# Macaron block on one core: the state loops of a selective scan interleaved by group, the state sum moved from TensorE to GpSimd, the experts' weights streamed

## The chip, the cores and the metric

The kernel runs on one core of a Trainium2 chip. Its time is the device time of one execution in microseconds; the median of three runs before the change is 2610.5 us (2609.67 to 2610.94). The core has five instruction queues: TensorE (PE, matmuls; PEld is its weight load), VectorE (DVE), ScalarE (ACT), GpSimd (POOL) and SyncE (SP), which here issues every DMA. Each runs its own instructions in order and waits on semaphores for the others. SBUF is the on-chip memory, PSUM the eight banks that TensorE writes.

## The reference, cut to what matters

Input x is 16 sequences of 256 tokens, 128 channels, float32. Six parts follow one another, each added to x, each on a layer norm of x:

```
x = x + 0.5 * ffn_fp4(layernorm(x))        # 128 -> 352 -> 128, inputs and hidden values quantised in blocks of 16
x = x + mamba(layernorm(x))                # two layers
x = x + 0.5 * ffn_fp4(layernorm(x))
x = x + 0.5 * experts(layernorm(x))        # 8 experts, 128 -> 512 -> 128, each weighted by a gate
x = x + attention(layernorm(x))            # 16 heads of 8, causal, relative bias
x = x + 0.5 * experts(layernorm(x))

# one mamba layer, ED = 256 channels, N = 16 states each:
xi, z = split(rmsnorm(h) @ in_w.T);  u = silu(causal_conv4(xi))
dr, B, C = split(u @ xp_w.T);        delta = softplus(dr @ dtw.T + dtb)
for t in tokens:
    state = exp(delta[t] * A) * state + delta[t] * B[t] * u[t]      # [256, 16]
    y[t]  = sum over the 16 states of state * C[t]
h = h + ((y + Dp * u) * silu(z)) @ out_w.T
```

## The kernel before, in words

**Tiling.** The batch is cut into 8 groups of 2 sequences, 512 tokens each. A group's x lies in SBUF as [128, 4, 128]; a ring of XR = 5 groups is kept, and SP loads group g + 5 when group g is stored (`c_sp`). In the Mamba layers channels lie on the partitions and the 512 tokens along the row: 256 channels are two halves of 128.

**The state loop.** One pass is one layer of one group: 16 passes. Its loop has 32 steps (2 halves x 16 states). A step s is: TensorE spreads row B[s] over 128 partitions into PSUM (L748); VectorE multiplies it by delta * u (L700); ScalarE makes exp(delta * A) (L818); VectorE runs the recurrence over the tokens with one scan instruction into the ring `hst` of RS = 3 buffers (L706); SP has loaded row C[s] from DRAM, spread over 128 partitions, into the ring `cring` of RC = 4 (L849); GpSimd multiplies state by C into the ring `prod` of RP = 4 (L829), and after each odd step adds two products (L834). TensorE sums the eight pairs of a half in PSUM with identity matmuls (L758). A scan waits for the product three steps back, since they share a buffer of `hst`; the B row of a step waits for the scan two steps back.

**The way into a loop** (`mamba_dve`, `mamba_pe`, `mamba_act` ahead of the step loop): rms norm, transposes, in-projection (L727), convolution on VectorE (L629), u, silu(z), B and C rows (L732, B split into three bfloat16 parts), delta by softplus (L738, L659, L664, L673, L676) and delta * u (L680). It uses the three PSUM banks of lane a. **The way out** is `half_end` for each half, y + Dp * u from the PSUM sum (L686) times silu(z) (L690), then the out-projection (L764) and its addition to hm (L715); after layer 1, GpSimd adds hm to x (L1220). In a group all of this is one after the other: way in, loop, way out, layer by layer, and the next group's after it.

**Lanes.** Lane a is the Mamba part, group after group. Lane b is everything on the b banks, in `b_order` (L410 to L415): parts (0, g) and (1, g) are the two FFNs of group g, (2, g) its attention. Lane c is the two expert passes of each group in `moe_order` (L409 to L414). FFN quantisation is VectorE's (`quantize_dve`, L483 to L505); GpSimd does its last multiplication (L517). An expert pass has the up matmuls (L912), ScalarE's relu (L947), the down matmuls (L920), ScalarE's weighting (L955) and GpSimd's addition to x (L971), eight experts in turn.

**What sets the order.** Each lane is a Python generator that yields after each step, for each engine. `merge` (L118) draws steps from the lanes as a string tells it, written out for each engine (ORDER_PE, ORDER_DVE, ...): "b2d8b" is two steps of b, eight of d, one of b. On TensorE "d" is one warming matmul of 128 columns by the identity (`warm_pe`, L1351) into a bank of lane c; it may only stand where no expert pass is under way. ORDER_PE has 1816 of them. No engine can leave this order at run time.

**Weights.** `w1` and `w2` of all eight experts, 2 MB each, are loaded once at the start and stay in SBUF.

## Time and profile before

| | |
|---|---|
| median of three runs | 2610.5 us |
| profiled execution, its time | 2610.92 us |
| its span, first to last instruction | 2609.1 us |
| mean granted TensorE clock, share of full | 0.957 |
| busy: PE, DVE, ACT, POOL | 2392.5, 1866.3, 1559.5, 1368.1 us |
| GpSimd adds hm to x (a group leaves the Mamba part): first, last | 282.5, 2207.5 us |
| DMA moved | 175.30 MB, mean 67 GB/s |

A page of the profile is one execution. Busy time is the time in which an engine had an instruction under way. A group is all instructions of one line on one engine and shape; a group's row gives their busy time and the mean of one, then the engine's idle time just before them and what ended it. An fp32 matmul shows as two records, so L758's 512 records are 256 calls.

### The profile page before, as it was taken

What the parts mean: (1) busy time and instruction counts of PE and PEld (TensorE: products, weight loads), DVE (VectorE), ACT (ScalarE), POOL (GpSimd) and SP (SyncE); (2) the same over time, 40 slices, a digit from 0 to 9 for tenths busy, and PEclk for the clock granted to TensorE, in tenths of its full rate; (3) what the DMA queues carried; (4) which work ended last, traced back from release to release, by engine and by line L of the source; (5) the groups of instructions that cost most, each with busy time, mean ns of one, the idle gap of its engine ahead of it and who ended that gap; (6) DMA issues with size and microseconds to landing.
All of it is one profiled execution on the core that took longest, in us unless ns stands there. A gap on an engine that the chain in (4) does not pass through costs nothing.

```text
span 2609.1 us, 40448 instructions
## 1 busy us (share of the span) xinstructions
PE 2392.5 (92%) x14313; PEld 1680.7 (64%) x14313; DVE 1866.3 (72%) x3817; ACT 1559.5 (60%) x3377; POOL 1368.1 (52%) x1227
## 2 busy tenths in 40 slices
PE   7999997997898999889898989999898999988988
PEld 7878884685565666656565656666575656666675
DVE  5879797789587978698687968797879777322220
ACT  1424435543686558664886668665876685566654
POOL 1466483947373856558373847476564737212001
PEclk9999998998899999999899999999999999989999
DMA  4123131312220222112230222121311422100100
GB/s 152 56 76 108 48 97 37 101 46 85 79 90 31 82 86 93 37 63 76 90 90 30 89 86 86 41 79 65 105 54 58 126 60 71 34 20 1 49 5 5
DMA packets 97640, 175.30 MB, mean 67 GB/s; under 512 B 11957, under 2 KB 23133, under 8 KB 95646
## 3 DMA queue, kind: packets, MB, share of 16 engines
q1 hardware_dynamic: 97438, 172.71, 21.6%
q8 instruction: 113, 1.85, 0.3%
q14 instruction: 89, 0.73, 0.1%
HBM read 157.44 MB, written 15.23 MB: 66 GB/s over the span
## 4 chain that ended last, share of the span: by engine, by line
PE 66%; DVE 12%; ACT 11%; POOL 6%; issue 5%; DMA 0%; SPq 0%; POOLq 0%; DVEq 0%; ACTq 0%
PE c_bank L912 15%; PE c_bank L920 14%; PE c_bank L1351 8%; PE a_bank L758 7%; PE a_bank L748 3%; PE b_bank L1060 3%; DVE hst L706 2%; POOL prod_c L829 2%; PE a_bank L727 2%; PE b_bank L580 2%; PE b_bank L1050 1%; ACT weighted_y L955 1%; POOL prod_c L834 1%; PE b_bank L1099 1%; PE b_bank L561 1%
## 5 line engine op out<-in xcount | busy, mean ns | idle before, releaser
L829 POOL TENSOR_TENSOR prod_c<-hst,prod_c 128x512 f32<-128x512 f32 x512 | 670.9, 1318 | 382.0 <-DVE hst L706 362.4
L706 DVE TENSOR_TENSOR_SCAN hst<-dA,a_bank 128x512 f32<-128x512 f32 x512 | 621.1, 1213 | 9.6
L920 PEld LDWEIGHTS c_bank<-w,hid 128*128 128x128 f32 x4096 | 506.8, 196 | 75.7 <-ACT hid L947 38.6
L912 PE MATMUL c_bank<-c_xT,w 128*128 128x512 f32 x1024 | 534.4, 628 | 21.7 <-ACT hid L947 12.1
L920 PE MATMUL c_bank<-w,hid 128*128 128x128 f32 x4096 | 523.0, 280 | 7.6 <-ACT hid L947 7.5
L818 ACT ACTIVATE dA<-delta,a_neg 128x510 f32<-128x510 f32 x512 | 365.2, 719 | 269.1 <-DVE hst L706 260.4
L1351 PEld LDWEIGHTS c_bank<-ident 128*128 128x128 f32 x3632 | 439.1, 194 | 36.1 <-issue 27.2
L1351 PE MATMUL c_bank<-ident 128*128 128x128 f32 x3632 | 445.3, 277 | 1.7 <-ACT weighted_y L955 1.7
L947 ACT ACTIVATE hid<-c_bank,b 128x512 f32<-128x512 f32 x512 | 349.6, 687 | 150.8 <-PE c_bank L912 148.8
L971 POOL TENSOR_TENSOR xs<-xs,weighted_y 128x512 f32<-128x512 f32 x128 | 166.2, 1298 | 426.3 <-ACT weighted_y L955 424.7
L700 DVE TENSOR_TENSOR a_bank<-du,a_bank 128x512 f32<-128x512 f32 x512 | 348.5, 681 | 37.1 <-PE a_bank L748 35.6
L834 POOL TENSOR_TENSOR prod_c<-prod_c 128x512 f32<-128x512 f32 x256 | 341.1, 1332 | 15.4
L912 PEld LDWEIGHTS c_bank<-c_xT,w 128*128 128x128 f32 x1024 | 177.6, 196 | 207.4 <-ACT hid L947 95.7
L1017 DVE CUSTOM_DVE_ANT_0 att_buf<-b_bank,bias 128x256 f32<-128x256 f32 (+1 forms) x512 | 153.7, 353 | 203.6 <-PE b_bank L1050 198.5
L758 PE MATMUL a_bank<-prod_c,ident 128*128 128x512 f32 x512 | 276.0, 621 | 17.8 <-POOL prod_c L834 16.7
L748 PE MATMUL a_bank<-bc,sel 128*128 128x512 bf16 x512 | 199.3, 396 | 53.5 <-DVE hst L706 41.4
L955 ACT ACTIVATE weighted_y<-c_bank,gw 128x128 f32<-128x128 f32 x512 | 153.4, 367 | 143.6 <-PE c_bank L920 143.3
L1140 ACT ACTIVATE pT<-b_bank 128x384 f32<-128x384 f32 x256 | 125.0, 488 | 68.1 <-PE b_bank L1060 66.3
L1060 PEld LDWEIGHTS b_bank<-ident,att_buf 128*128 128x128 f32 x768 | 97.6, 150 | 99.8 <-issue 62.9
L1060 PE MATMUL b_bank<-ident,att_buf 128*128 128x128 f32 x768 | 137.3, 291 | 26.1 <-ACT pT L1140 15.9
L1131 ACT ACTIVATE att_buf<-att_buf,nmx 128x256 f32<-128x256 f32 x256 | 129.8, 507 | 29.6 <-DVE nmx L1017 29.2
L517 POOL TENSOR_TENSOR b_hq<-ffn_buf,b_quant_scales 128x704 f32<-128x704 f32 x32 | 44.9, 1404 | 190.6 <-DVE ffn_buf L505 190.6
(177 smaller groups left out, 2814.5 us busy)
## 6 DMA issues: line engine op xcount, KB each, us to landing
prod_c<-c_rows SPq DMA_DIRECT2D x512, 256.0 KB, 3.2
q_and_k<-qk_rows SPq DMA_DIRECT2D x64, 192.0 KB
qk_rows<-att_buf SPq DMA_DIRECT2D x40, 256.0 KB, 2.6
w<-in_w SPq DMA_DIRECT2D x2, 2048.0 KB
xs<-in_x SPq DMA_DIRECT2D x8, 256.0 KB, 6.7
bias<-skew SPq DMA_DIRECT2D x1, 2048.0 KB, 8.0
qk_rows<-b_xn SPq DMA_DIRECT2D x8, 256.0 KB, 3.0
out_dram<-xs SPq DMA_DIRECT2D x8, 256.0 KB, 2.4
```

Source lines behind the costliest of these rows:

```text
L700: nc.vector.tensor_tensor(b_bank, du[:, h, :], b_bank, ALU.mult).then_inc(M.dBx.sem, 1)
L706: nc.vector.tensor_tensor_scan(hst[:, s % RS, :], dA[:, s % RA, :], b_bank, 0.0, ALU.mult, ALU.add).then_inc(M.h.sem, 1)
L748: nc.tensor.matmul(S.bank[2 - s % 2 * 2][:, :], sel[:, s % NST, :], bc3[:, :], start=True, stop=True).then_inc(M.b.sem, 1)
L758: nc.tensor.matmul(S.bank[1][:, :], ident[:, :], prod[:, 2 * k % RP, :], start=(k % (NST // 2) == 0), stop=(k % (NST // 2) == NST // 2 - 1 ...
L818: nc.scalar.activation(half_batches(dA[:, s % RA, :], 1), half_batches(delta[:, h, :], 1), ACT.Exp, scale=a_neg[:, l, h, n:n + 1]).then_in ...
L829: nc.gpsimd.tensor_tensor(prod[:, s % RP, :], hst[:, s % RS, :], cring[:, s % RC, :], ALU.mult).then_inc(M.pp.sem, 1)
L834: nc.gpsimd.tensor_tensor(prod[:, (s - 1) % RP, :], prod[:, (s - 1) % RP, :], prod[:, s % RP, :], ALU.add).then_inc(M.pair.sem, 1)
L912: nc.tensor.matmul(S.bank[up_bank(e, c)][:, :], w1[:, e, c * 128:(c + 1) * 128], S.xT[:, :], start=True, stop=True).then_inc(M.up.sem, 1)
L920: ins = nc.tensor.matmul(S.bank[down_bank(f)][:, t * D:(t + 1) * D], hid[:, f % 2, j, t * 128:(t + 1) * 128], w2[:, f, j, :], start=(j == ...
L947: nc.scalar.activation(hid[:, e % 2, c, :], S.bank[up_bank(e, c)][:, :], ACT.Relu, bias=b1[:, e, c:c + 1]).then_inc(M.relu.sem, 1)
L1060: ins = nc.tensor.transpose(S.bank[2][:, j * 128:(j + 1) * 128], pr[:, m % 4, j * 128:(j + 1) * 128], ident[:, :])
L1351: nc.tensor.matmul(sc_.bank[0][:, 0:128], ident[:, :], ident[:, :], start=True, stop=True)
```

## The change

Lane a now holds only the state loops, numbered k = 0 to 15, in the order of `loops`: (0,0), (0,1), (1,0), (2,0), (1,1), (3,0), (2,1), ... (7,0), (6,1), (7,1), each (group, layer). So from the third loop on, neighbouring loops mostly belong to different groups. A new lane d holds the ways in ("gap") and out ("end"), in the order of `between`, and uses one PSUM bank, bank 1; a step there waits until the one before has been read. u, sz, delta, du and bc3 are doubled, hm is threefold, y has a tile of its own. The half-end of the second half moves from the loop to lane d. The softplus takes its maximum from PSUM before the logarithm is there.

The state sum: for each state after the first of a half GpSimd adds the product to `acc` in SBUF; the first is written there directly. The identity matmuls (L758) and the pair additions (L834) are gone, and `half_end` reads `acc` in place of a PSUM bank. RP is 3, XR is 6.

The experts' weights: `w1` and `w2` have two buffers of one expert each; SP loads 256 KB for each of both for every expert of all 16 expert passes (256 loads), each once the matmuls that used the buffer are done, drawn between the C rows by ORDER_SP, together with the stores and loads of x. b_order runs one FFN further ahead, (0, g + 3) in place of (0, g + 2).

All five order strings are new. ORDER_PE has 2181 warming calls (now "e"). After the last step of lane a, ORDER_PE had 157 steps of b, 272 of c and 97 warming calls; it has 209, 322 and 58.

The core of the diff; lines removed from functions that are printed above are mostly left out.

```diff
@@ -34,92 +34,98 @@
 EXP_MASK = 0x7F800000
 MAGIC = 1.5 * 2.0 ** 22
 BELOW = 1.0 - 2.0 ** -24
-XR = 5
+XR = 6
 PT = 6
-RS, RA, RP, RC = 3, 3, 4, 4
+RS, RA, RP, RC = 3, 3, 3, 4
+LOOPS = GROUPS * LAYERS
...
-        w1 = sb("w1", [128, EXPERTS, HID])
+        w1 = sb("w1", [128, 2, HID])
         b1 = sb("b1", [128, EXPERTS, HC])
-        w2 = sb("w2", [128, EXPERTS, HC, D])
+        w2 = sb("w2", [128, 2, HC, D])
...
-        yT = xc
+        yT = sb("yT", [128, HALVES, TOK])
+        acc = sb("y_sum", [128, HALVES, TOK])
...
-        b_order = [(0, 0), (0, 1), (1, 0), (0, 2)]
+        b_order = [(0, 0), (0, 1), (0, 2), (1, 0), (0, 3)]
         for g in range(1, GROUPS):
             moe_order += [(0, g), (1, g - 1)]
-            b_order += [(1, g), (0, g + 2), (2, g - 1)]
+            b_order += [(1, g), (0, g + 3), (2, g - 1)]
...
+        loops = [(0, 0), (0, 1), (1, 0)]
+        for g in range(2, GROUPS):
+            loops += [(g, 0), (g - 1, 1)]
+        loops.append((GROUPS - 1, 1))
...
+        def half_end(dve, L, M, k, h):
+            l, q = place(k)[1], k % 2
+            dve.wait_ge(M.acc.sem, L.at(M.acc, (h + 1) * (NST - 1)))
+            if h == 0 and k:
+                dve.wait_ge(M.proj.sem, k)
+            nc.vector.scalar_tensor_tensor(out=yT[:, h, :], in0=u[:, q, h, :], scalar=chan[:, 1, l, h:h + 1],
+                                           in1=acc[:, h, :], op0=ALU.mult, op1=ALU.add).then_inc(M.yD[h].sem, 1)
+            yield
+            dve.wait_ge(M.yD[h].sem, L.at(M.yD[h], 1))
+            nc.vector.tensor_tensor(yT[:, h, :], yT[:, h, :], sz[:, q, h, :], ALU.mult).then_inc(M.y[h].sem, 1)
+            yield
+        def loop_dve(dve, L, S, M, k):
+            q = k % 2
+            L.g = k
             for s in range(STEPS):
                 h, n = s // NST, s % NST
+                b_bank = S.bank[2 - s % 2 * 2][:, :]
+                if n == 0:
+                    dve.wait_ge(M.du.sem, L.at(M.du, h + 1))
                 dve.wait_ge(M.b.sem, L.at(M.b, s + 1))
+                nc.vector.tensor_tensor(b_bank, du[:, q, h, :], b_bank, ALU.mult).then_inc(M.dBx.sem, 1)
                 yield
                 dve.wait_ge(M.dBx.sem, L.at(M.dBx, s + 1))
                 dve.wait_ge(M.dA.sem, L.at(M.dA, s + 1))
+                if k * STEPS + s >= RS:
+                    dve.wait_ge(M.pp.sem, k * STEPS + s - RS + 1)
+                nc.vector.tensor_tensor_scan(hst[:, (k * STEPS + s) % RS, :], dA[:, (k * STEPS + s) % RA, :], b_bank, 0.0,
                                              ALU.mult, ALU.add).then_inc(M.h.sem, 1)
                 yield
+                if s == NST + 5:
+                    yield from half_end(dve, L, M, k, 0)
+        def end_dve(dve, L, S, M, k):
+            L.g = k
+            yield from half_end(dve, L, M, k, 1)
             dve.wait_ge(M.proj.sem, L.at(M.proj, 1))
+            nc.vector.tensor_tensor(hm[:, place(k)[0] % 3, :, :], hm[:, place(k)[0] % 3, :, :], S.bank[1][:, :].rearrange("p (t d) -> p t d", d=D),
                                     ALU.add).then_inc(M.added.sem, 1)
             yield
...
+            for j in range(4):
+                if 1 <= j <= 2:
+                    pe.wait_ge(M.conv.sem, L.at(M.conv, j))
+                elif j == 3:
+                    pe.wait_ge(M.sz.sem, L.at(M.sz, 1))
...
+        def loop_pe(pe, L, S, M, k):
+            L.g = k
             pe.wait_ge(M.bcS.sem, L.at(M.bcS, 1))
+            for s in range(STEPS):
+                if k * STEPS + s >= 2:
+                    pe.wait_ge(M.h.sem, k * STEPS + s - 1)
+                nc.tensor.matmul(S.bank[2 - s % 2 * 2][:, :], sel[:, s % NST, :], bc3[:, k % 2, :],
+                                 start=True, stop=True).then_inc(M.b.sem, 1)
+                yield
...
+        def loop_pool(pool, L, M, k):
+            L.g = k
+            def product(s):
+                h, n, i = s // NST, s % NST, k * STEPS + s
+                pool.wait_ge(s_c[i % RC], 16 * (i // RC + 1))
+                pool.wait_ge(M.h.sem, i + 1)
+                if n == 0 and k:
+                    pool.wait_ge(M.yD[h].sem, k)
+                if n > RP:
+                    pool.wait_ge(M.acc.sem, L.at(M.acc, h * (NST - 1) + n - RP))
+                elif n and h:
+                    pool.wait_ge(M.acc.sem, L.at(M.acc, NST - 1))
+                elif n and k:
+                    pool.wait_ge(M.acc.sem, 2 * (NST - 1) * k)
+                nc.gpsimd.tensor_tensor(prod[:, s % RP, :] if n else acc[:, h, :], hst[:, i % RS, :], cring[:, i % RC, :],
+                                        ALU.mult).then_inc(M.pp.sem, 1)
+                yield
+            def added(s):
+                h, n = s // NST, s % NST
+                if n:
+                    pool.wait_ge(M.pp.sem, L.at(M.pp, s + 1))
+                    done = h * (NST - 1) + n - 1
+                    if n > 1:
+                        pool.wait_ge(M.acc.sem, L.at(M.acc, done))
+                    nc.gpsimd.tensor_tensor(acc[:, h, :], acc[:, h, :], prod[:, s % RP, :], ALU.add).then_inc(M.acc.sem, 1)
+                    yield
+            for s in range(STEPS + 1):
+                if s < STEPS:
+                    yield from product(s)
+                if s:
+                    yield from added(s - 1)
+        def loop_sp(sp, L, M, k):
+            L.g = k
+            sp.wait_ge(s_cst, 16 * (k + 1))
             for s in range(STEPS):
+                i = k * STEPS + s
+                if i >= RC:
+                    sp.wait_ge(M.pp.sem, i - RC + 1)
+                row = bass.AP(c_dram.tensor, (k * NST + s % NST) * TOK, [[0, 128], [1, TOK]])
+                sp.dma_start(cring[:, i % RC, :], row).then_inc(s_c[i % RC], 16)
                 yield
...
+                        if c == 0:
+                            pe.wait_ge(s_w1[e % 2], 16 * ((L.g * EXPERTS + e) // 2 + 1))
+                        nc.tensor.matmul(S.bank[up_bank(e, c)][:, :], w1[:, e % 2, c * 128:(c + 1) * 128], S.xT[:, :],
...
         def c_sp(sp, L):
-            for g in range(GROUPS):
-                sp.wait_ge(moe.acc.sem, moe.acc.per * (moe_order.index((1, g)) + 1))
-                sp.dma_start(out[g * TOK:(g + 1) * TOK, :].rearrange("(t p) d -> p t d", p=128), x_of(g)).then_inc(s_out, 16)
-                yield
-                if g + XR < GROUPS:
-                    sp.wait_ge(s_out, 16 * (g + 1))
-                    load_x(sp, g + XR)
-                    yield
+            stored = 0
+            for n in range(EXPERTS * len(moe_order) + 2):
+                if n < EXPERTS * len(moe_order):
+                    if n >= 2:
+                        sp.wait_ge(moe.up.sem, HC * (n - 1))
+                    sp.dma_start(w1[:, n % 2, :], a["w1"][:, n % EXPERTS, :]).then_inc(s_w1[n % 2], 16)
+                    yield
+                    if n >= 2:
+                        sp.wait_ge(moe.down.sem, n - 1)
+                    sp.dma_start(w2[:, n % 2, :, :], a["w2"][:, n % EXPERTS, :, :]).then_inc(s_w2[n % 2], 16)
+                    yield
+                if n % EXPERTS == 1 and n > EXPERTS and moe_order[n // EXPERTS - 1][0]:
+                    g = moe_order[n // EXPERTS - 1][1]
+                    sp.wait_ge(moe.acc.sem, moe.acc.per * (n // EXPERTS))
+                    sp.dma_start(out[g * TOK:(g + 1) * TOK, :].rearrange("(t p) d -> p t d", p=128), x_of(g)).then_inc(s_out, 16)
+                    stored += 1
+                    yield
+                    if g + XR < GROUPS:
+                        sp.wait_ge(s_out, 16 * stored)
+                        load_x(sp, g + XR)
+                        yield
```

## Rows read from the trace of the kernel before

**Rows 1.** The page: busy us, share and instructions; the chain that ended last.
```profile
PE 2392.5 (92%) x14313; PEld 1680.7 (64%) x14313; DVE 1866.3 (72%) x3817; ACT 1559.5 (60%) x3377; POOL 1368.1 (52%) x1227
...
PE 66%; DVE 12%; ACT 11%; POOL 6%; issue 5%; DMA 0%; SPq 0%; POOLq 0%; DVEq 0%; ACTq 0%
```

**Rows 2.** Windows: PE, PEld, DVE, ACT, POOL busy us, PEclk, DMA share, GB/s.
```profile
0.00:98.00 98.00, 81.14 (x594) 72.69 (x595) 62.54 (x132) 31.80 (x70) 17.40 (x30) 1.00 0.34 113
98.00:2206.00 2108.00, 1948.91 (x11435) 1356.14 (x11434) 1713.30 (x3253) 1299.14 (x2777) 1287.60 (x1125) 0.96 0.24 74
2206.00:2609.00 403.00, 362.42 (x2289) 251.85 (x2287) 90.47 (x434) 228.56 (x531) 63.06 (x73) 0.94 0.07 19
450.00:500.00 50.00, 49.56 (x236) 30.79 (x236) 44.46 (x49) 32.79 (x62) 46.62 (x38) 0.99 0.37 111
600.00:650.00 50.00, 37.54 (x185) 24.17 (x184) 48.89 (x73) 18.37 (x33) 38.59 (x31) 0.86 0.28 84
1750.00:1800.00 50.00, 48.30 (x283) 35.03 (x282) 47.25 (x59) 25.16 (x54) 42.95 (x35) 1.00 0.25 79
```

**Rows 3.** Groups of the page: busy us, mean ns, idle before, releaser.
```profile
L829 POOL TENSOR_TENSOR prod_c<-hst,prod_c 128x512 f32<-128x512 f32 x512 | 670.9, 1318 | 382.0 <-DVE hst L706 362.4
L706 DVE TENSOR_TENSOR_SCAN hst<-dA,a_bank 128x512 f32<-128x512 f32 x512 | 621.1, 1213 | 9.6
L912 PE MATMUL c_bank<-c_xT,w 128*128 128x512 f32 x1024 | 534.4, 628 | 21.7 <-ACT hid L947 12.1
L920 PE MATMUL c_bank<-w,hid 128*128 128x128 f32 x4096 | 523.0, 280 | 7.6 <-ACT hid L947 7.5
L1351 PE MATMUL c_bank<-ident 128*128 128x128 f32 x3632 | 445.3, 277 | 1.7 <-ACT weighted_y L955 1.7
L700 DVE TENSOR_TENSOR a_bank<-du,a_bank 128x512 f32<-128x512 f32 x512 | 348.5, 681 | 37.1 <-PE a_bank L748 35.6
L834 POOL TENSOR_TENSOR prod_c<-prod_c 128x512 f32<-128x512 f32 x256 | 341.1, 1332 | 15.4
L758 PE MATMUL a_bank<-prod_c,ident 128*128 128x512 f32 x512 | 276.0, 621 | 17.8 <-POOL prod_c L834 16.7
```

**Rows 4.** Windows of L1351 alone: PE and PEld busy us.
```profile
98.00:2206.00 2108.00, 362.90 (x2958) 358.93 (x2959) 0.96 0.24 74
2206.00:2609.00 403.00, 24.11 (x193) 22.43 (x191) 0.94 0.07 19
```

**Rows 5.** Timeline of POOL in a loop alone: start us, us.
```profile
257.85 2.50 POOL L829 TENSOR_TENSOR prod_c<-hst,prod_c 128x512 f32<-128x512 f32 x2
...
260.43 1.27 POOL L834 TENSOR_TENSOR prod_c<-prod_c 128x512 f32<-128x512 f32 x1
```

**Rows 6.** Window from loop 0's end to loop 1's first step, as rows 2.
```profile
184.00:211.00 27.00, 26.90 (x189) 22.45 (x188) 13.56 (x21) 16.66 (x33) 1.21 (x2) 1.00 0.12 41
```

**Rows 7.** Waits: us in total, times, longest us.
```profile
POOL prod_c L829 <- DVE hst L706: 362.4, 169, 27.0
...
DVE xc L686 <- PE a_bank L758: 45.7, 12, 5.9
...
POOL prod_c L829 <- DMA prod_c<-c_rows: 14.3, 2, 11.0
```

**Rows 8.** Timeline of two SBUF inputs beside POOL, and L492's shortest, median, longest.
```profile
335.43 1.27 POOL L829 TENSOR_TENSOR prod_c<-hst,prod_c 128x512 f32<-128x512 f32 x1 [0.72 <-DVE hst L706]
...
335.76 1.68 DVE L492 TENSOR_TENSOR ffn_buf<-att_buf,b_quant_scales 128x704 f32<-128x704 f32 x1
336.77 1.80 POOL L834 TENSOR_TENSOR prod_c<-prod_c 128x512 f32<-128x512 f32 x1
...
L492 DVE TENSOR_TENSOR ffn_buf<-att_buf,b_quant_scales x32: 860/892/1952, 39.1 to 2243.1; 128x704 f32<-128x704 f32 x32
```

**Rows 9.** SP's loads of the C rows: issue ns, and us to landing.
```profile
L849 SPq DMA_DIRECT2D prod_c<-c_rows x512: 319/320/854, 88.6 to 2188.7; - x171
...
DMA to landing us min/median/max: 2.9/3.2/11.3
```

More of the change, by code:

```diff
@@ L288, in build @@
         s_cst = plain("c_rows_in_dram")
+        s_w1 = [plain(f"up_weights_loaded_{i}") for i in range(2)]
+        s_w2 = [plain(f"down_weights_loaded_{i}") for i in range(2)]
         s_qkd = plain("q_and_k_in_dram")
@@ L616, in half_batches, with place, gaps_and_ends @@
             return ap.rearrange("p (b s) -> p b s", b=GB)[:, :, k:]
-        def mamba_dve(dve, L, S, M, l):
-            N = M.norm
-            step = [0, 0]
-            for k in range(1, KCONV):
-                for h in range(HALVES):
-                    if k == 1:
+        loops = [(0, 0), (0, 1), (1, 0)]
+        for g in range(2, GROUPS):
+            loops += [(g, 0), (g - 1, 1)]
+        loops.append((GROUPS - 1, 1))
+        def place(k):
+            return loops[k]
+        def gaps_and_ends():
+            todo, ended = [], 0
+            for k, (g, l) in enumerate(loops):
+                due = max(k - 1, loops.index((g, 0)) + 1 if l else 0)
+                while ended < due:
+                    todo.append(("end", ended))
+                    ended += 1
+                todo.append(("gap", k))
+            return todo + [("end", k) for k in range(ended, LOOPS)]
```

532 lines of the change are left out of this document (264 added, 268 removed).

## The prediction

> **What bounds the kernel now.** The page first: TensorE is busy 2392.5 of 2609.1 us and has 66% of the chain that ended last [rows 1]. The groups then say what that busy time is: 445.3 us of it are the warming matmuls of L1351, which no result needs, and 276.0 us the state sum of L758 [rows 3]. So TensorE is full, but not with work. The windows show three parts [rows 2]: a way in until the first scan (98 us), the stage of the state loops (98 to 2206 us), and a tail of 403 us with neither scan nor GpSimd product, where TensorE is busy 362.4 us. In the stage VectorE is busy 1713.3 of 2108 us (81%), GpSimd 1287.6 (61%), TensorE 1948.9, less 362.9 of warming [rows 4], that is 75% with work.
>
> A state loop with nothing beside it runs at GpSimd's pace: two products in 2.50 us and a pair addition to 1.27 us, 3.8 us for two steps [rows 5]; VectorE needs 0.68 + 1.21 us a step [rows 3]. Between two loops of a group VectorE is busy 13.56 us and GpSimd 1.21 us of the 27 us from 184 to 211 [rows 6]: that is the gap which the change fills. In the stage GpSimd waits 362.4 us for the state, and VectorE 45.7 us for the last state sum [rows 7].
>
> **The change, part by part.** I sum over the stage, as a bill for each engine, and put the first loop and the tail beside it. There are 16 passes (loop with its ways in and out).
>
> *State sum off TensorE.* 256 calls (512 records of L758) go: 276.0 us of busy time. On GpSimd 256 pair additions become 30 additions in each pass, 480 in all: 224 more of 1.27 us, 285 us. Its stage bill goes from 1287.6 to 1573 us. A pass then has 32 products and 30 additions, 62 x 1.27 = 79 us, where it had 48, 61 us.
>
> *Interleaving.* From pass 2 on, a pass's way in belongs to another group and can lie under the loop before it. Nothing is removed by that; it allows VectorE to go from 81% to what its dense stretches reach: 48.89 of 50 us (98%) from 600, 47.25 (95%) from 1750 [rows 2]. Pass 1 still needs pass 0 of the same group, so one gap stays open: 27 us [rows 6], 30 us with all ways in on one bank, where each matmul now waits for the reader of the one before. Elsewhere I cost this longer chain at nothing, since a loop of 80 us or more covers it; bare, it would cost at most VectorE's idle time of such a gap once more, 27 - 13.56 = 13 us a pass, up to 215 us in all [rows 6].
>
> *SBUF inputs beside GpSimd.* This is the cost that decides. While GpSimd is inside a product, a VectorE operation with two SBUF inputs waits: L492 takes 1.68 us at 335.76 beside L829, and 0.86 at its shortest; the GpSimd addition behind it then takes 1.80 us in place of 1.27 [rows 8]. A pass has 29 such operations: 10 in the way in, 4 on the way out (L686 now reads the sum from SBUF and not from PSUM), 15 in an FFN's quantisation. Before, the ways in and much of the FFN ran while GpSimd stood idle. If GpSimd is busy 85% of the time, and the wait is on average half of its 1.27 us, that is 29 x 0.85 x 0.64 = 16 us a pass, less some 4 us that the mean durations hold already (L829 and L834 are 0.05 us over 1.27 in the mean, and VectorE's share is like it): 12 us, 195 us in all. The bounds: 0 (the orders place them where GpSimd waits) and 29 x 0.82 = 24 us, less 4: 320 us (each as at 335.76). I take 195, between them. GpSimd loses as much again.
>
> The Trainium skill has this as a rule ("SBUF — State Buffer", section "SBUF: two separate sides"): VectorE with two SBUF inputs and GpSimd share one port pair under an exclusive lock held for a whole instruction, so that the loser blocks fully. The trace agrees (1.68 us against 0.86, rows 8). The rule speaks against this change, since it moves work onto GpSimd and VectorE's SBUF operations beside it.
>
> *The stage's sum.* VectorE: 1713.3, less 26 us of attention work that moves into the tail, plus 195: 1882 us. At 96% (between the 95 and the 98 above) 1960 us, plus the open gap of 30: 1990. GpSimd would have 1573 + about 200 in it, 89%; it reached 46.62 of 50 us (93%) from 450 [rows 2], so VectorE bounds, narrowly. TensorE with work: 1586 less 276 less 62, 63%: free.
>
> *Tail.* Counted in the written orders, TensorE has after the last state-loop step now 4 expert passes, 2 attentions and an FFN (272 and 157 steps); after the change 322 and 209, with 58 warming calls in place of 97, so 50 of the 68 steps of one expert pass and 52 of the 70 of an attention more, and 39 calls fewer. An expert pass is (534.4 + 523.0) / 16 = 66 us [rows 3]; the tail's 362.4 us less four of them less 24.1 of warming [rows 2, 4] leave 74 for two attentions and an FFN, some 30 each. So 66 x 50/68 + 30 x 52/70 - 39 x 0.245 = 62 us, at the tail's share (90%) 69. Tail 472 us. Below, 30 us if it fills idle time; above, 85.
>
> *Streamed weights.* 256 loads of 256 KB replace two of 2 MB. SP issues one in 0.32 us, such a load lands in 3.2 us [rows 9], and a buffer comes free one expert (66/8 = 8 us) before its use. Cost 0 when SP is on time. But SP is one queue in order: a load that waits for an expert's matmul holds the C rows behind it, of which the ring has four, 4 x 2.53 = 10 us. Bounds 0 and 11.3 - 3.2 = 8 us (its longest landing) for a third of the 128 experts, 340 us; I take 0, the nearest row being that products waited for this queue only twice in 512 [rows 7]. With fewer bytes before it the way in is shorter or the same; a third group's FFN goes into it: 98 becomes 100 us.
>
> **Sum.** 100 + 1990 + 472 = 2562 us of span; the profiled execution took 1.8 us more than its span and is 0.4 above the median of 2610.5. I say 2560.
>
> **Rivals.**
> (a) *The forecast*, VectorE bound with lock waits: 2560, own range 2510 to 2605. Chance 0.38.
> (b) *The waits for the port stay small and the overlap holds*: VectorE 1687 us at 94% (the 95% stretch) 1795, plus 30; 100 + 1825 + 472 = 2397. TensorE gives the same: 2392.5 - 276.0 + 365 more warming calls in the new order x 0.245 = 2206 us, at the present 92% 2405. For it: from 1750 VectorE, GpSimd and TensorE are all near full together (47.25, 42.95, 48.30 of 50) [rows 2]. Against: rows 8. With all between it and (a), 2390 to 2510: 0.22.
> (c) *GpSimd becomes the bound*: 79 us of loop, (1287.6 - 1012) / 16 = 17 of other work, 29 x 0.85 x 0.89 = 22 of waiting for VectorE's SBUF operations, 118 us a pass. VectorE waits for the product three steps back, and GpSimd for the scan, so each one's stall returns to the other. At the 86% of the stretch from 1750 that is 137 us a pass, 2195 + 30, in all 2797; at 90%, 131 us, 2700. It decides once a pass takes over (2609 - 100 - 472 - 30) / 16 = 125 us, that is GpSimd under 94% with these waits. For it: GpSimd never stood above 93% [rows 2]. Against: the waits are counted on both sides, while one side's wait frees the other. I give it 2620 to 2720, chance 0.30. By the skill's rule alone, with every one of the 29 blocked, this would be the outcome; its time is the one given here.
> (d) *SP's queue starves the products*: a third of the 128 experts at 8 us, of which half is covered: 2560 + 170 = 2730. Chance 0.05. (e) *The overlap doesn't come about* because the orders, written for other durations, make each way in wait: the gap of 27 us stays in half of the passes, 2560 + 7 x 27 = 2750, of which 130 falls away again (two thirds of the 195, since GpSimd then idles): 2620. Chance 0.05.
>
> **How the numbers follow.** The likeliest single case is (a), so 2560. Faster holds (b) and nearly all of (a), 0.59; within 0.2% (5 us, about what a measurement of this kernel can tell from no change) 0.07, from the edges of (a), (c) and (e); slower 0.34, (c), (d) and a little of (a). The range for 8 in 10 runs from the middle of (b), 2440, to 2690, which leaves out the upper end of (c). Both signs hold much of the chance; (a)'s own range stands above.
>
> **What would show it.** L758 and its idle times gone; an addition on GpSimd of 480 records. Mean durations of the VectorE operations with two SBUF inputs (L492, L501, L664, L680, L690) well above those before, and of GpSimd's products above 1.32 us: 12 us a pass in sum for (a), next to none for (b). VectorE at 94% or more of the stage with the first and last scan some 1990 us apart. For (c) GpSimd is above 90% and VectorE's waits are for products; for (d) products wait for the C rows; for (e) VectorE waits for its ways in. The tail should take 472 us. The prediction is wrong if TensorE's chain still ends the stage, if the port costs nothing, or if the tail grows by less than 30 us.

## The result: slower, with the profile after

The changed kernel takes 2673.4 us (median of 4 runs, 2668.7 to 2683.9) against 2610.2 us (the kernel before, now four runs): a ratio of 1.0245 [1.0231, 1.0258], 63 us slower. The forecast was 2560 us, so faster.

The page after gives busy us, share and instructions, then the chain that ended last. It answers to [rows 1].
```profile
PE 2296.8 (86%) x14381; PEld 1678.7 (63%) x14531; DVE 1948.8 (73%) x3817; ACT 1572.8 (59%) x3387; POOL 1672.6 (63%) x1451
...
PE 46%; DVE 19%; ACT 12%; issue 9%; POOL 5%; DMA 1%; another core or an unknown queue 0%; SPq 0%; POOLq 0%; DVEq 0%; ACTq 0%
```
TensorE's part of the chain fell from 66% to 46%, and no single engine took its place: VectorE has 19%. The windows after, with the columns of [rows 2]: the way in, the stage, the tail, then the stretch between the first and the last scan in two parts (from the first scan of pass 0 to the first of pass 6, and from there to the last scan), and three stretches of the early part.
```profile
0.00:114.00 114.00, 95.45 (x713) 86.23 (x716) 74.11 (x157) 35.27 (x81) 21.30 (x36) 1.00 0.24 72
114.00:2195.00 2081.00, 1769.47 (x10911) 1295.13 (x11057) 1761.70 (x3100) 1256.91 (x2641) 1573.98 (x1331) 0.92 0.32 98
2195.00:2671.00 476.00, 431.91 (x2760) 297.37 (x2759) 112.97 (x564) 280.60 (x668) 77.30 (x85) 0.94 0.19 57
111.50:806.50 695.00, 562.29 (x3550) 442.24 (x3599) 620.95 (x799) 312.28 (x582) 552.71 (x449) 0.88 0.27 81
806.50:2197.80 1391.30, 1211.94 (x7393) 856.45 (x7490) 1144.77 (x2311) 948.14 (x2069) 1024.65 (x888) 0.94 0.35 106
550.00:600.00 50.00, 23.31 (x77) 12.91 (x78) 38.79 (x45) 20.67 (x43) 44.33 (x40) 0.60 0.35 99
600.00:650.00 50.00, 30.03 (x99) 15.05 (x100) 46.34 (x48) 21.46 (x36) 44.43 (x35) 0.64 0.35 107
650.00:700.00 50.00, 16.82 (x39) 6.83 (x39) 46.86 (x58) 21.17 (x42) 43.53 (x37) 0.53 0.24 74
```
The kernel before, cut at the same two places:
```profile
98.30:843.10 744.80, 689.94 (x4268) 517.07 (x4266) 608.05 (x996) 371.83 (x750) 448.89 (x387) 0.96 0.24 73
843.10:2195.10 1352.00, 1248.45 (x7088) 829.80 (x7089) 1102.15 (x2253) 924.73 (x2021) 832.11 (x732) 0.96 0.25 76
```
From 550 to 700 GpSimd is busy 44 of 50 us and TensorE 17 to 30, at a granted clock of 0.53 to 0.64. Over the whole stage VectorE is busy 1761.7 of 2081 us, 84.7%. In [rows 2] it was 81%; 96% were forecast.

For a split that needs no choice of borders, take each kernel's first and last scan (name, ns at least/median/most, start of the first to start of the last). Before:
```profile
L706 DVE TENSOR_TENSOR_SCAN hst<-dA,a_bank x512: 1152/1220/1222, 98.3 to 2195.1; 128x512 f32<-128x512 f32 x171
```
After:
```profile
L760 DVE TENSOR_TENSOR_SCAN hst<-dA,a_bank x512: 1153/1212/1223, 111.5 to 2197.8; 128x512 f32<-128x512 f32 x171
```
The way in is 13.2 us longer, the stretch from first to last scan 10.5 us shorter (2086.3 against 2096.8), and what follows the last scan 59.5 us longer (473.5 against 414.0): +62.2 of span. So the tail came near its forecast (+69), and the stage didn't shrink by 118 us but by some 10. These 10 us are a difference of two parts: passes 0 to 5 became 50 us shorter (695 against 745), passes 6 to 15 became 39 us longer (1391 against 1352). VectorE's idle time between the same marks fell from 137 to 74 us in the early passes. In the late passes it did not fall (250 and 246 us), while VectorE's busy time there rose by 43 us. So the new lanes filled VectorE's idle time in the early passes only.

The groups that answer to [rows 3]:
```profile
L935 POOL TENSOR_TENSOR prod_c<-hst,prod_c 128x512 f32<-128x512 f32 x480 | 644.1, 1343 | 221.2 <-issue 169.9
L946 POOL TENSOR_TENSOR y_sum<-y_sum,prod_c 128x512 f32<-128x512 f32 x480 | 647.2, 1348 | 1.6
L760 DVE TENSOR_TENSOR_SCAN hst<-dA,a_bank 128x512 f32<-128x512 f32 x512 | 619.7, 1210 | 38.7 <-POOL prod_c L935 26.5
L1036 PE MATMUL c_bank<-c_xT,w 128*128 128x512 f32 x1024 | 544.3, 638 | 26.1 <-ACT weighted_y L1080 12.8
L1463 PE MATMUL c_bank<-ident 128*128 128x128 f32 x4362 | 540.2, 279 | 13.8 <-DVE hst L760 11.8
L1045 PE MATMUL c_bank<-w,hid 128*128 128x128 f32 x4096 | 504.6, 277 | 7.9 <-ACT hid L1072 6.3
```
L758 is gone, and L946 has 480 records, as the change says.

### The profile page after: what moved, and what is told of

It reads as the page before. It is cut to its first block, busy times and chain, and to the rows that moved or that the text cites. A ratio compares the mean times of both kernels' runs of the same rounds, so it can differ in the third digit from the quotient of the medians.

```text
span 2671.3 us, 41985 instructions
## 1 busy us (share of the span) xinstructions
PE 2296.8 (86%) x14381; PEld 1678.7 (63%) x14531; DVE 1948.8 (73%) x3817; ACT 1572.8 (59%) x3387; POOL 1672.6 (63%) x1451
## 4 chain that ended last, share of the span: by engine, by line
PE 46%; DVE 19%; ACT 12%; issue 9%; POOL 5%; DMA 1%; another core or an unknown queue 0%; SPq 0%; POOLq 0%; DVEq 0%; ACTq 0%
PE c_bank L1036 13%; PE c_bank L1045 13%; DVE hst L760 6%; PE c_bank L1463 4%; DVE a_bank L754 3%; PE b_bank L1185 3%; POOL y_sum L946 2%; ACT weighted_y L1080 2%; PE a_bank L792 1%; ACT dA L900 1%; PE b_bank L1175 1%; POOL prod_c L935 1%; PE b_bank L592 1%; ACT hid L1072 1%; PE b_bank L1224 1%
## 5 line engine op out<-in xcount | busy, mean ns | idle before, releaser
L935 POOL TENSOR_TENSOR prod_c<-hst,prod_c 128x512 f32<-128x512 f32 x480 | 644.1, 1343 | 221.2 <-issue 169.9
L946 POOL TENSOR_TENSOR y_sum<-y_sum,prod_c 128x512 f32<-128x512 f32 x480 | 647.2, 1348 | 1.6
L760 DVE TENSOR_TENSOR_SCAN hst<-dA,a_bank 128x512 f32<-128x512 f32 x512 | 619.7, 1210 | 38.7 <-POOL prod_c L935 26.5
L1036 PE MATMUL c_bank<-c_xT,w 128*128 128x512 f32 x1024 | 544.3, 638 | 26.1 <-ACT weighted_y L1080 12.8
L1463 PE MATMUL c_bank<-ident 128*128 128x128 f32 x4362 | 540.2, 279 | 13.8 <-DVE hst L760 11.8
L1463 PEld LDWEIGHTS c_bank<-ident 128*128 128x128 f32 x4362 | 533.5, 196 | 24.1 <-issue 16.6
L1045 PEld LDWEIGHTS c_bank<-w,hid 128*128 128x128 f32 x4096 | 485.2, 193 | 56.9 <-ACT hid L1072 38.8
L1045 PE MATMUL c_bank<-w,hid 128*128 128x128 f32 x4096 | 504.6, 277 | 7.9 <-ACT hid L1072 6.3
L1142 DVE CUSTOM_DVE_ANT_0 att_buf<-b_bank,bias 128x256 f32<-128x256 f32 (+1 forms) x512 | 152.1, 353 | 230.7 <-PE b_bank L1175 230.2
L816 PE MATMUL a_bank<-bc,sel 128*128 128x512 bf16 x362 | 148.5, 418 | 137.8 <-DVE hst L760 133.5
L816 PEld LDWEIGHTS a_bank<-bc,sel 128*128 128x128 bf16 x512 | 51.0, 100 | 248.3 <-DVE hst L760 205.8
```

What stands on the lines that cost most here:

```text
L760: nc.vector.tensor_tensor_scan(hst[:, (k * STEPS + s) % RS, :], dA[:, (k * STEPS + s) % RA, :], b_bank, 0.0, ALU.mult, ALU.add).then_inc(M ...
L816: nc.tensor.matmul(S.bank[2 - s % 2 * 2][:, :], sel[:, s % NST, :], bc3[:, k % 2, :], start=True, stop=True).then_inc(M.b.sem, 1)
L935: nc.gpsimd.tensor_tensor(prod[:, s % RP, :] if n else acc[:, h, :], hst[:, i % RS, :], cring[:, i % RC, :], ALU.mult).then_inc(M.pp.sem, 1)
L946: nc.gpsimd.tensor_tensor(acc[:, h, :], acc[:, h, :], prod[:, s % RP, :], ALU.add).then_inc(M.acc.sem, 1)
L1036: nc.tensor.matmul(S.bank[up_bank(e, c)][:, :], w1[:, e % 2, c * 128:(c + 1) * 128], S.xT[:, :], start=True, stop=True).then_inc(M.up.sem, 1)
L1045: ins = nc.tensor.matmul(S.bank[down_bank(f)][:, t * D:(t + 1) * D], hid[:, f % 2, j, t * 128:(t + 1) * 128], w2[:, f % 2, j, :], start=(j ...
```

## The experiments

Kernels whose labels begin with e are the changed kernel with one edit, those with b are the kernel before with one edit. "The time" is the median, set against the 2673.4 of the changed kernel for e and against the kernel before of the same chip (2610.0 to 2611.4) for b. Four theories on where the stage's gain went are named in the expectations. Q: loads of weights hold up the C rows in SP's queue. P: GpSimd, by its longer loop and the SBUF port that it shares with VectorE, sets the pace. I: GpSimd paces the early passes, TensorE's experts the late ones and the tail. O: no engine bounds alone; the written orders do.

**e1_no_stream.** The streaming taken away: two experts' weights are loaded once and serve all eight.
```diff
-                    if n >= 2:
-                        sp.wait_ge(moe.up.sem, HC * (n - 1))
-                    sp.dma_start(w1[:, n % 2, :], ...)
+                    if n < 2:
+                        sp.dma_start(w1[:, n % 2, :], ...)
```
(and so for w2; TensorE waits only for the first load of each buffer.)


> Changed kernel without the streaming: two experts' weights are loaded once and serve all eight (the other six experts' weights are left out), so SP issues no load that waits for an expert's matmul. Theory Q (SP's one queue in order: a weight load that waits holds the C rows behind it, and GpSimd stands idle 191 us before its products with no releaser shown): most of these 191 us go, the idle time named issue before L935 falls below 40 us, and the time falls by 100 to 190 us, to 2490 to 2570. Theory P (the port and GpSimd's load): GpSimd idles elsewhere instead, time within 20 us of 2673. Theory O (the written orders fit none of the real durations, so a stall removed in one place returns in another): 10 to 60 us less.


Measured: 2663.8 us (2660.2 to 2674.0), 1.0211 [1.0188, 1.0233] of before, 10 less than the changed kernel, which is at the edge of what these runs can tell apart. In the changed kernel SP waits behind experts' down matmuls for 598.9 us in 121 waits, and it costs next to nothing. GpSimd's waits before its products, 169.9 us marked "issue" in the changed kernel, stay. Changed kernel (us in total, times, longest us):
```profile
POOL prod_c L935 <- issue: 169.9, 72, 12.9
...
SPq L1488 <- PE c_bank L1045: 598.9, 121, 11.9
```
and without streaming:
```profile
POOL prod_c L935 <- issue: 167.8, 72, 12.4
```
Rival (d) falls. The trace also says what these waits are, the longest one first (start us, us):
```profile
784.30 1.21 DVE L760 TENSOR_TENSOR_SCAN hst<-dA,a_bank 128x512 f32<-128x512 f32 x1
785.65 1.77 POOL L935 TENSOR_TENSOR prod_c<-hst,prod_c 128x512 f32<-128x512 f32 x1 [12.86 <-issue]
```
Each of the 77 products before which the idle time is marked "issue" (the 72 above and five that write `y_sum`, 191 us together) starts 0.13 to 0.14 us after the end of the scan that it multiplies. So GpSimd waited there for VectorE, as before the change, and not for a C row: theory Q falls by this too.

**e4_act_queue.** The same loads issued by ScalarE.
```diff
+ (behind the last relu of an expert)
+   act.dma_start(w1[:, n % 2, :], a["w1"][:, n % EXPERTS, :])
+ (behind the wait for its down product)
+   act.dma_start(w2[:, n % 2, :, :], a["w2"][:, n % EXPERTS, :, :])
```


> Changed kernel, all its loads kept, but ScalarE issues the weight loads, at the point where it has just waited for the same matmuls anyway; SP has only the C rows, x, q and k, and the output. Theory Q: as without streaming, 2490 to 2570, plus up to 256 x 0.33 = 85 us of issue time on ScalarE, which is 59% busy; so 2500 to 2600. Theory that the traffic itself costs (89 GB/s where it was 67): no better than 2673. Theory P: within 20 us of 2673.


Measured: 2697.2 us (2692.3 to 2702.0), 24 more. SP was the better place for them, and theory Q, which asked for 2500 to 2600, falls again.

**e2_narrow_adds.**
```diff
-  nc.gpsimd.tensor_tensor(acc[:, h, :], acc[:, h, :], prod[:, s % RP, :], ALU.add)
+  nc.gpsimd.tensor_tensor(acc[:, h, 0:16], acc[:, h, 0:16], prod[:, s % RP, 0:16], ALU.add)
```


> Changed kernel with GpSimd's 480 additions over 16 of the 512 columns (the sum of the other 496 columns is left out). Takes some 1.1 us x 480 = 520 us off GpSimd and with it most of the blocking of VectorE's operations with two SBUF inputs. Theory P: the time falls by 100 us or more, to 2570 or less, and L693, L738, L742 come back to about 0.70 us each. Theory Q: the products still wait for C rows, since SP still stands behind the experts; under 40 us less. Theory O: 20 to 60 us less.


Measured: 2601.6 us (7 runs), 72 less; against before 0.9966 [0.9954, 0.9978]. GpSimd's busy time fell by 513 us (1672.6 to 1159.4) and VectorE's by 90 (1948.8 to 1859.3). Passes 0 to 5 give 42 us (first scans of passes 0 and 6: 695.0 us apart with full additions, 653.1 with narrow ones), passes 6 to 15 give 35 (1391 and 1356), and with the tail that is the 77 us by which the two profiled executions differ; passes 10 to 14 alone keep their lengths within 5 us each. L693 falls from 1442 to 1021 ns in the mean, L738 from 1266 to 989 and L742 from 1059 to 841, not to the 700 that theory P asked for. The time lies 32 us above P's 2570 and 12 under what theory O allowed (60 us less).

**e3_no_warm.** No warming matmuls (L1463).
```diff
-                nc.tensor.matmul(sc_.bank[0][:, 0:128], ident[:, :], ident[:, :], start=True, stop=True)
```


> Changed kernel without its 2181 warming calls on TensorE. If they stand in the way of work (TensorE's queue is in order, 540 us of warming where 445 were): 20 to 60 us faster. If the clock that they hold is worth more than their room: slower than 2673, by more the further the granted clock falls below 0.924; I expect 2720. Under Q and P alike no large change.


Measured: 2735.2 us, 62 more, at a mean granted clock of 0.809 in place of 0.924. The warming still pays, but it does not hold the clock from 550 to 700 of the changed kernel: TensorE is busy 17 to 30 of 50 us there, and its granted clock of 0.53 to 0.64 is mostly the lower of its two levels (1.2 GHz). What this low clock cost the early passes, no run separates.

**e5_half_up, b2_half_up.** The experts' up matmuls over half the columns, in both kernels.
```diff
-  nc.tensor.matmul(S.bank[up_bank(e, c)][:, :], w1[...], S.xT[:, :],
+  nc.tensor.matmul(S.bank[up_bank(e, c)][:, 0:256], w1[...], S.xT[:, 0:256],
```


> Changed kernel, the experts' up matmuls over 256 of the 512 columns (half of the up product is left out): some 270 us less TensorE work, 17 us in each expert pass. Theory I (two limits in turn: passes 1 to 9 are bound by the loop's own engines, GpSimd and VectorE; passes 10 to 14 and the tail by TensorE's expert work, which the interleaving pushed back): passes 1 to 5 keep their lengths within 5 us, the tail of 476 us loses 60 to 80, passes 10 to 14 of 146 us lose 15 to 25 each; in all 150 to 200 us less. Theory O (no engine bounds, the fixed orders do): under 100 us less, spread evenly.

> The kernel before with the same cut of the up matmuls (half of the up product is left out). If TensorE bounded the passes from 6 on and the tail: 17 us a pass for the 16 expert passes, of which four lie in the tail: 150 to 230 us less than 2610. If the time before was set by the written order: under 100.


**e6_narrow_du, b3_narrow_du.** VectorE's multiply ahead of the scan over 64 of 512 columns, in both.
```diff
-  nc.vector.tensor_tensor(b_bank, du[:, q, h, :], b_bank, ALU.mult)
+  nc.vector.tensor_tensor(b_bank[:, 0:64], du[:, q, h, 0:64], b_bank[:, 0:64], ALU.mult)
```


> Changed kernel, VectorE's multiplication of the B row over 64 of 512 columns (the rest of that product is left out): 0.47 us x 512 = 240 us off VectorE. My forecast had VectorE as the bound of the whole stage; if it is, the time falls by 150 us or more. Theory I: GpSimd's 2.5 us a step bounds the early passes and TensorE the late ones, so under 50 us. Theory O: 50 to 100.

> The kernel before with VectorE's multiplication over 64 of 512 columns (left out as in e6): 240 us off VectorE. TensorE bound: under 50 us less than 2610. VectorE bound: 150 or more.


**e8_narrow_relu.** ScalarE's relu of the experts over 64 of 512 columns from the second group on.
```diff
-  nc.scalar.activation(hid[:, e % 2, c, :], S.bank[up_bank(e, c)][:, :], ACT.Relu, ...)
+  w = TOK if L.g == 0 else 64
+  nc.scalar.activation(hid[:, e % 2, c, 0:w], S.bank[up_bank(e, c)][:, 0:w], ACT.Relu, ...)
```


> Changed kernel with ScalarE's relu of the experts (L1072, 512 instructions, mean 689 ns) over 64 of 512 columns from the second group on; the rest of hid keeps old data. It removes about 240 us of ScalarE's busy time and shortens each up-relu-down chain. Theory L (late passes and the tail are bound by the latency of the chain up, relu, down between TensorE and ScalarE, not by TensorE's columns): as much as halving the up matmuls gave, 40 to 60, so 2615 to 2635, with the late passes 10 to 14 shorter. Theory I (TensorE's own work bounds them): at most 10 to 20, 2655 to 2665. Theory O without a preference: 0.1 to 0.3 of 240, 2600 to 2650.


Measured, with the busy time taken away (its group for TensorE, its engine for the others):

| kernel | removed, us | time, us | gain | gain per us removed |
|---|---|---|---|---|
| e5_half_up | TensorE 197 | 2616.0 | 57 | 0.29 |
| b2_half_up | TensorE 203 | 2535.0 | 76 | 0.37 |
| e6_narrow_du | VectorE 212 | 2641.6 | 32 | 0.15 |
| b3_narrow_du | VectorE 209 | 2587.2 | 24 | 0.11 |
| e8_narrow_relu | ScalarE 165 | 2645.1 | 28 | 0.17 |
| e2_narrow_adds | GpSimd 513 | 2601.6 | 72 | 0.14 |

Nothing that is taken away gives back more than 0.37 of itself, on any engine, in either kernel. So in neither is one engine the bound, which speaks for O. My own forecast had VectorE as the bound of the stage and so asked for 150 us or more from e6: it gave 32. Theory I had asked for 150 to 200 from e5, 60 to 80 of it in the tail, and has the places right but not the sizes: passes 0 to 5 lose 4 us, passes 6 to 15 lose 36, what follows the last scan 17. Theory L, named for e8 (the chain from up matmul over relu to down matmul bounds the late passes), asked for 40 to 60 and got 28. With half the up matmuls gone, TensorE's idle time ahead of them grows from 26.1 to 62.5 us, half of it for the relu. In e5_half_up:
```profile
L1036 PE MATMUL c_bank<-c_xT,w 128*128 128x256 f32 x1024 | 347.0, 440 | 62.5 <-ACT hid L1072 31.6
```
**e7_narrow_and_half.** e2 and e5 together.


> Changed kernel with both reliefs: GpSimd's additions over 16 of 512 columns and the experts' up matmuls over 256 of 512 columns. Alone they gave 72 and 57. If the early passes (GpSimd) and the late ones with the tail (TensorE's experts) are separate stages: 2673 - 129 = 2544, within 8. If both relieve one shared bound, so that what one gives the other can't: 2590 to 2600. If each uncovers the other (an order in which both had to be late): 2500 or less.


Measured: 2530.2 us, 143 less, where the two alone give 129. The separate stages of the expectation ask for 2544 within 8, so this is nearest but missed by 14, and the places do not bear it out: cut at the same scans, e7 loses 49 us in passes 0 to 5, 72 in passes 6 to 15 and 18 after them. In each part that is about the sum of the two alone (42 and 4, 35 and 36, 1 and 17). So both reliefs work in the late passes, and neither takes anything from the other.

The second question was what the move of the sum costs without the new lanes. It is answered in the old structure.

**b1_narrow_sum**: the state sum nearly free. **b5_sum_moved**: b1, and GpSimd with an additional addition of 512 columns a pair. **b4_pool_adds**: that addition alone.
```diff
-  nc.tensor.matmul(S.bank[1][:, :], ident[:, :], prod[:, 2 * k % RP, :],
+  nc.tensor.matmul(S.bank[1][:, 0:16], ident[:, :], prod[:, 2 * k % RP, 0:16],
...
+  nc.gpsimd.tensor_tensor(acc2[:, :], acc2[:, :], prod[:, (s - 1) % RP, :], ALU.add)
```


> Kernel before with TensorE's state-sum matmuls (L758) over 16 of 512 columns; the sum is then wrong. Nearly all of L758's 276.0 us on TensorE goes, GpSimd keeps its pair additions. This is what the removal of the sum from TensorE can give in the old structure. Theory O (a fixed written order in which no engine bounds alone; every relief gives a third or less of what it removes): 2610 - 0.3 x 265 = 2530. Theory I (TensorE bounds the late passes and the tail): 2610 - 0.7 x 265 x (1403/2108) = 2490, with the gain in passes 6 to 15. No effect (above 2600): the state sum's matmuls lay in gaps that were idle anyway, and the change removed nothing of worth.

> Kernel before in its old structure, with both sides of the move: TensorE's state-sum matmuls over 16 of 512 columns, and on GpSimd a second full addition behind each pair addition, so that GpSimd does 32 operations of 512 columns per half loop as in the changed kernel (31). The sum's value is wrong. The move alone, without the new lanes. The structure's part of the change is then 2673 less this. Theory P (a heavier GpSimd costs about what narrowing its additions gave back in the changed kernel, 72): 72 above the kernel with only the narrow matmuls, so 2600 to 2610, and the new structure is worth nothing or costs 60. Rival (in the old structure the loop runs alone for part of each pass, and GpSimd's 2.6 us per step there adds 0.6 us x 32 x 16 = 300 at most, half of it seen): 2700, and the new structure saved 30 to 100 that the sum gave away.

> Kernel before with only GpSimd's additional 256 additions of 512 columns (341 us more on GpSimd, TensorE's sum kept). Theory P: 2610 + 72 = 2680. Rival (the loop at GpSimd's pace for the whole of each pass): 2750 and more. If GpSimd's idle time (about 34% of the span before) takes it all: under 2630. Against the kernel with both sides it says what TensorE's relief is worth once GpSimd is loaded: theory O, 60 to 80.


Measured: b1 2561.9 us, 0.9813 [0.9798, 0.9828]; b5 2779.9, 1.0649 [1.0633, 1.0665]; b4 2797.9, 1.0718 [1.0701, 1.0735]. For b1 theory O's 2530 is nearest, and still 32 below. Theory P missed b5 and b4 by far, and their rivals have the direction (2700 asked of b5, 2750 and more of b4): the heavier GpSimd costs 218 us here (b5 less b1), three times the 72 that narrowing all additions gives back in the changed kernel. GpSimd in b5, with the loop alone (start us, us):
```profile
241.25 2.50 POOL L830 TENSOR_TENSOR prod_c<-hst,prod_c 128x512 f32<-128x512 f32 x2
243.83 1.27 POOL L835 TENSOR_TENSOR prod_c<-prod_c 128x512 f32<-128x512 f32 x1
245.18 1.27 POOL L839 TENSOR_TENSOR acc<-acc,prod_c 128x512 f32<-128x512 f32 x1
246.40 2.50 POOL L830 TENSOR_TENSOR prod_c<-hst,prod_c 128x512 f32<-128x512 f32 x2
```
Two steps take 5.15 us where they took 3.8 [rows 5]; with it the chain of waits has GpSimd at 31% (6% in [rows 1]) and TensorE at 34%:
```profile
PE 34%; POOL 31%; DVE 13%; issue 11%; ACT 9%; DMA 0%; POOLq 0%; SPq 0%; DVEq 0%; ACTq 0%
```

Put together with first and last scans of each trace (us):

| | first scan at | passes 0 to 5 | passes 6 to 15 | first to last scan | after it | time |
|---|---|---|---|---|---|---|
| old lanes, sum nearly free (b1) | 98.3 | 734 | 1317 | 2051 | 413 | 2561.9 |
| old lanes, sum on TensorE (before) | 98.3 | 745 | 1352 | 2097 | 414 | 2610.2 |
| old lanes, sum on GpSimd (b5) | 98.7 | 817 | 1444 | 2261 | 418 | 2779.9 |
| new lanes, sum nearly free (e2) | 111.9 | 653 | 1356 | 2009 | 473 | 2601.6 |
| new lanes, sum on GpSimd (after) | 111.5 | 695 | 1391 | 2086 | 474 | 2673.4 |

"New lanes" stands for all that the change does besides moving the sum, the streamed weights included. The change is then two changes of opposite sign. Moving the sum costs 170 us in the old lanes; the new lanes give back 107 with the sum on GpSimd, and cost 40 where the sum is nearly free. They shorten the stage by 42 or by 175 us, and pay 13 at the start and 56 to 60 at the end for it. Where the sum is nearly free they shorten only passes 0 to 5 (by 81 us) and lengthen passes 6 to 15 (by 39). The rows are not matched in all: b1 keeps the 256 full pair additions on GpSimd (341 us of busy time), which e2 does not have, and b5 keeps narrow matmuls on TensorE (99.5 us) and makes 512 additions where the changed kernel makes 480. Estimate: the pair additions' 28 us (b7 below) would put b1 at some 2534, and the cost of the new lanes there at some 67 us in place of 40. The new lanes with the sum on TensorE were not tried: the eight PSUM banks are taken.

**b7_narrow_pairs**: GpSimd's pair additions over 16 of 512 columns. **b6_sum_on_pe**: no additions on GpSimd, TensorE sums all 512 products; the opposite of the change.
```diff
 (b6, TensorE)
-  pe.wait_ge(M.pair.sem, L.at(M.pair, k + 1))
+  pe.wait_ge(M.pp.sem, L.at(M.pp, 2 * k + 2))
+  nc.tensor.matmul(S.bank[1][:, :], ident[:, :], prod[:, (2 * k + 1) % RP, :], ...)
 (b6, GpSimd; in b7 it stays, over [:, 0:16])
-  nc.gpsimd.tensor_tensor(prod[:, (s - 1) % RP, :], prod[:, (s - 1) % RP, :], prod[:, s % RP, :], ALU.add)
```


> Kernel before with GpSimd's 256 pair additions (L834, 341.1 us) over 16 of 512 columns; the sum is then wrong. About 265 us less on GpSimd. Theory G (GpSimd paces the old structure's state loop in every pass already, 218 us lost for 341 added): the same slope down, 0.64 x 265 = 170 less, 2440. Rival K (there is a knee: VectorE's multiply and scan bound the loop once GpSimd has less than one and a half operations a step): 2580 to 2610.

> Kernel before with no additions on GpSimd: TensorE sums all 512 products itself (512 matmuls of 512 columns in place of 256, 276 us more on TensorE, 341 less on GpSimd). The computation is whole. Theory G: 170 to 218 less from GpSimd, 50 more from TensorE (what narrowing its sum gave, 48): 2440 to 2490, faster than both kernels. Rival K: 2610 - 15 + 50 = 2645. Theory I carried over (TensorE bounds the late passes and the tail): 2610 + 0.7 x 276 x 0.67 - 20 = 2720.


Measured: b7 2583.8 us, 0.9894 [0.9879, 0.9909]; b6 2766.2, 1.0597 [1.0582, 1.0613]. Theory G falls, rival K holds for b7. For b6 K's price of TensorE's extra matmuls (50) was far too low: theory I's 2720 is nearest, and is still 46 short. TensorE's windows in b6, of the stage and the tail:
```profile
98.00:2360.00 2262.00, 2121.29 (x11797) 1442.02 (x11947) 1696.07 (x3253) 1299.70 (x2777) 949.73 (x869) 0.97 0.23 69
2360.00:2764.00 404.00, 363.96 (x2287) 252.58 (x2285) 90.25 (x434) 227.96 (x531) 62.83 (x73) 0.93 0.07 18
```
So the kernel before stands at a corner. Off GpSimd a us gives 0.10 (b7: 27.6 of 268), onto it a us costs 0.56 to 0.65 (b4: 188 of 332; b5 less b1: 218 of 337). Off TensorE's state sum 0.25 (b1: 48 of 190), onto it 0.71 (b6 less b7: 182 of 258, L758 in b7 and L758 with L760 in b6, while GpSimd's 72 us of narrow additions go too). No run of the whole computation beat the kernel before.

## Why the prediction was wrong

**The step that failed** is in the stage's sum: "VectorE: ... 1882 us. At 96% (between the 95 and the 98 above) 1960 us". The bill was too high and the share far too high. VectorE's busy time in the stage came to 1762 us, and 1762 at 96% plus the open gap of 30 would have been 1865 us; it took 2081, at 84.7%. The 96% was read from two stretches of 50 us [rows 2] and given to 2108. The written order of each engine has to be met step by step. That this is why the share stays low is argued; shown is that with every relief giving 0.10 to 0.37 and the relief of VectorE itself 0.15 (e6), the stage is not the bill of its busiest engine divided by a share. The overlap that was to raise the share came in passes 0 to 5 alone: VectorE's share rose from 82% to 89% there, and only from 81.5% to 82.3% in passes 6 to 15, which the change made 39 us longer. TensorE had not more work to do there: without warming its busy time fell from 1169 to 1046 us, while warming rose from 79 to 166. Nor does one wait: of VectorE's 246 us of idle time in them the largest item is 65.5 us, attention's L1142 waiting for TensorE (us in total, times, longest us, from 807 to 2198):
```profile
DVE att_buf L1142 <- PE b_bank L1175: 65.5, 54, 4.5
```
What ends each step of passes 6 to 15 stays open beyond that. The doses say only that the bound is shared, with TensorE's experts giving most.

**State sum off TensorE.** The counts were right (480 additions, GpSimd's busy time up 304.5 us, forecast 285). The worth was not. I priced the removal through TensorE's bill, as free of effect, and the addition through GpSimd's bill, as hidden under VectorE's. In the old lanes they are worth -48 and +218 us (b1, b5 less b1). In the new lanes all of GpSimd's additions cost 72 (e2).

**SBUF inputs beside GpSimd.** 195 us were forecast; VectorE's busy time rose by 82.5 us over the whole span, and narrow additions take 90 away again. So it is under half of the forecast, and its size is not uniform as I had it. Four groups carry most: L693 (mean 1442 ns, where the same step took 692), L738 (1266 against 735), L717 (974 against 721), L708 (1127 against 808). The 15 operations of an FFN's quantisation, half of my 29, didn't change (L513 940 ns against 965, L517 896 against 930): they had stood beside GpSimd before, and their waits were, it seems, in the mean durations already. I had allowed 4 us a pass for that. My count also left out operations with one SBUF input, and some of them became longer as well: L714 takes 762 ns in the mean where it took 594, L498 560 against 428, L507 763 against 662. These three are 17 of the 82.5 us.

**Way in.** 100 us forecast, 111.5 measured at the first scan. "Elsewhere I cost this longer chain at nothing, since a loop covers it" is true but for pass 0, which has no loop over it. There the longer way in costs 13 us; how much of it is the one bank and how much the third group's FFN, no run separates.

**Tail.** 472 us forecast; 473.5 after the last scan, 476 in the window above. The terms counted in the written orders held nearly: +69 forecast, +59.5 between equal marks. This was the only loss that the orders show before a run. With the way in it is 73 us: more than the new lanes save in the stage where the sum is nearly free (42), and less than they save where it is on GpSimd (175).

**Streamed weights.** 0 forecast, about 10 measured (e1), at the edge of the noise.

**The rivals.** (c) named the size: its 2620 to 2720 holds the result. That is luck in part, since its conditions were not met. It wanted GpSimd above 90% with VectorE waiting for products: GpSimd is busy 1574 of 2081 us over the stage, 76%, and comes near 90% only in pass 4 and a little after (44 of 50 us), and the scans wait for products for 26.5 us in all (L760 above), while GpSimd waits for scans ten times as long. (b) fell by its overlap; of the port waits that it took for small, under half of (a)'s 195 came. (e), a failed overlap, is nearest for the late passes, which became 39 us longer; I gave it 0.05, as though 81% were an accident of the old lanes. Its sign, VectorE waiting for its ways in, is 31 of the 246 us of VectorE's idle time there. The range of 2440 to 2690 held the time only because it took in most of (c); the direction was wrong.

## What to carry to other kernels

Where the engines run fixed orders and each is at 75 to 90%, don't divide the busiest engine's bill by the share of its best stretch. Price each moved operation from both sides, since a kernel whose orders were fitted to it can stand at a corner, as this one does (0.10 to 0.37 of what is taken away, 0.56 to 0.71 of what is added). Price separately what a change removes, adds and reorders, as here -48, +218 and -107 us. Compare the kernels part by part, cut at the same instruction: a stage that shrank by 10 us was 50 us shorter and 39 us longer. And count, in the written orders, what is left after the last step of the stage: pushing groups back to overlap them lengthens the tail by what is pushed, and that is the one term that can be read before a run.
